# Cross-attention, two layers: the softmax shift's products of two key blocks and two heads in four groups of 32 rows

## What is computed

```
# layer 0: 16 heads of 64
h = layernorm(x, gamma, beta)
Q, K, V = h @ Wq, context @ Wk, context @ Wv
attn = softmax(Q K^T) * 64 ** -0.5
x = x + (attn V) @ Wo + bo
# layer 1: 16 heads of 32
xn = rmsnorm(x) * norm_w
q, k, v = rope and l2-normalise(xn @ wq, ctx @ wk), ctx @ wv
x = x + (softmax(q k^T * sqrt(32)) v) @ wout
```

## Time and profile before

| | us |
|---|---|
| median of 3 runs | 3376.78 |
| lowest and highest | 3375.62, 3377.91 |
| the profiled execution's own time | 3378.76 |
| its span | 3376.9 |
| TensorE busy | 3157.1 |
| VectorE busy | 2385.7 |
| ScalarE busy | 1404.2 |

### The profile page before, as it was taken

How to read it: one execution, slowest core, us unless ns; L and a number is a source line. 1 busy time by engine, 2 the same in 40 slices (tenths; PEclk the granted TensorE clock), 3 DMA queues, 4 the chain that set the end, 5 groups by cost and what they waited for, 6 DMA issues and landing times.

```text
span 3376.9 us, 51123 instructions
## 1 busy us (share of the span) xinstructions
PE 3157.1 (93%) x20448; PEld 1614.6 (48%) x20448; DVE 2385.7 (71%) x2805; ACT 1404.2 (42%) x1728; POOL 502.6 (15%) x221
## 2 busy tenths in 40 slices
PE   5999999899899999889999999998999999999897
PEld 3555555444355554544344555454434455545442
DVE  3667666787776676678776766667877767666877
ACT  1333333456433333355643333335563333334555
POOL 1000002342000000334100000034410000013440
PEclk8999999999999999999999999999999999999999
DMA  3001000101111010011111010101112010000001
GB/s 108 18 21 25 22 23 15 57 22 39 43 49 25 21 24 21 21 55 25 32 55 41 21 25 21 24 14 58 26 32 71 21 27 21 25 21 21 18 14 36
DMA packets 178322, 105.88 MB, mean 31 GB/s; under 512 B 81453, under 2 KB 147117, under 8 KB 178089
## 3 DMA queue, kind: packets, MB, share of 16 engines
q1 hardware_dynamic: 178088, 102.60, 11.4%
HBM read 93.12 MB, written 9.42 MB: 30 GB/s over the span
## 4 chain that ended last, share of the span: by engine, by line
PE 83%; DVE 8%; issue 4%; ACT 3%; DMA 1%; SPq 1%; DVEq 0%; POOL 0%; ACTq 0%; POOLq 0%
PE o_acc L654 19%; PE scores L642 19%; PE work L680 14%; PE work L676 11%; PE work L700 10%; PE work L610 5%; DVE acc L797 4%; PE work L694 3%; ACT probs L727 2%; DVE tile_max L778 1%; PE work L684 1%; DVE resid L882 1%; DVE stats L817 1%; PE work L710 0%; PE work L689 0%
## 5 line engine op out<-in xcount | busy, mean ns | idle before, releaser
L727 ACT ACTIVATE probs<-scores 128x1024 f32<-128x1024 f32 x1024 | 995.8, 1023 | 501.2 <-PE scores L642 462.1
L778 DVE TENSOR_REDUCE tile_max<-work 128x2 f32<-128x1024 f32 x496 | 607.0, 1224 | 557.4 <-PE work L610 554.0
L797 DVE TENSOR_TENSOR acc<-acc,probs 128x1024 f32<-128x1024 f32 x768 | 984.8, 1305 | 20.2 <-ACT probs L727 0.2
L654 PE MATMUL o_acc<-probs,v_tok 128*64 128x512 f32 (+1 forms) x4096 | 778.1, 611 | 0.1
L914 POOL TENSOR_TENSOR inv<-sumsq,power 128x16 f32<-128x16 f32 x64 | 233.0, 3640 | 2110.5 <-DVE sumsq L863 2110.5
L700 PE MATMUL work<-wo,o_sum 128*128 128x512 f32 x768 | 429.6, 647 | 39.7 <-issue 27.6
L642 PE MATMUL scores<-q_high,k_high 32*128 32x512 f16 (+1 forms) x2048 | 311.4, 394 | 71.0 <-ACT probs L727 47.3
L654 PEld LDWEIGHTS o_acc<-probs,v_tok 128*64 128x64 f32 (+1 forms) x4096 | 165.4, 122 | 349.1 <-issue 334.4
L882 DVE TENSOR_TENSOR resid<-work,resid 128x512 f32<-128x512 f32 x384 | 261.4, 684 | 65.3 <-PE work L700 65.2
L642 PE MATMUL scores<-q_high,k_low 32*128 32x512 f16 (+1 forms) x2048 | 305.4, 385 | 0.0
L642 PE MATMUL scores<-q_low,k_high 32*128 32x512 f16 (+1 forms) x2048 | 304.5, 384 | 0.0
(11 more groups left out here) (77 smaller groups left out, 2662.6 us busy)
## 6 DMA issues: line engine op xcount, KB each, us to landing
recip<-rows_dram SPq DMA_DIRECT2D x380, 64.0 KB, 2.1
stage<-in_x_dram SPq DMA_DIRECT2D x8, 1024.0 KB, 6.3
wq<-in_L_xattn_Wq_dram SPq DMA_DIRECT2D x32, 256.0 KB, 2.8
resid<-in_x_dram SPq DMA_DIRECT2D x8, 1024.0 KB, 5.4
wo<-in_L_xattn_Wo_dram SPq DMA_DIRECT2D x32, 256.0 KB, 2.7
out_dram<-resid SPq DMA_DIRECT2D x8, 1024.0 KB, 4.3
wk<-in_L_xattn_Wk_dram SPq DMA_DIRECT2D x32, 192.0 KB, 2.6
wv<-in_L_xattn_Wv_dram SPq DMA_DIRECT2D x32, 192.0 KB, 2.6
```

What stands on the lines that cost most here:

```text
L654: mm = pe.matmul(o_acc[h * d:(h + 1) * d, :], v_tok[par][:, kt, h * d:(h + 1) * d], probs[:, unit_slot(t, n, kt, h // 2), h % 2, :], start ...
L727: act.activation(probs[:, no % RING, :, :], scores[:, unit_banks(t, n, kt, u), :], ACT.Exp, scale=(1.0, float(D1) ** 0.5 / QK_SCALE ** 2)[ ...
L778: dve.tensor_reduce(tile_max[:, qt, :, n:n + 1], maxima_banks(e), AX.X, ALU.max, negate=True).then_inc(dve_freed, 1)
L797: dve.tensor_tensor(a[:, heads, :], before, probs[:, unit_slot(t, n, kt, u), :, :], ALU.add).then_inc(add_ok, 1)
```

## The change

In layer 0 the shift's products leave `products`. For every even block, that is once a step, `shift_pair` writes four of them ahead of the others: for block i (0 or 1) of the step and head h, rows 64h + 32i to 64h + 32i + 31 of `ones_r` and `shift`, into that block's and head's own bank. For this the row of `shift` with the maximum has to be there twice, at rows 0 and 32 and at rows 64 and 96; a second reduction on VectorE writes columns 32 and 96 of `neg_max`. The waits of both blocks for `exp_ok` stand ahead of the four products. Layer 1 is as before.

```
+            def shift_pair(t, n, kt):
+
+                for i in range(2):
+                    no = UNIT_NO[t, n, kt + i, 0]
+                    if no >= 2:
+                        pe.wait_ge(exp_ok, no - 1)
+                for i in range(2):
+                    for h in range(G0):
+                        r = slice(h * D0 + i * D1, h * D0 + (i + 1) * D1)
+                        pe.matmul(scores[:, 2 * (UNIT_NO[t, n, kt + i, 0] % 2) + h, :], ones_r[r, :], shift[t % 2][r, tokens(n)],
+                                  start=True, stop=False)
...
-                if units[-1] >= 2:
-                    pe.wait_ge(exp_ok, units[-1] - 1)
...
                 if l == 0:
-                    products = ((kh, qh), (kl, qh), (kh, ql), (None, shift[par]))
+                    if kt % 2 == 0:
+                        shift_pair(t, n, kt)
+                    products = ((kh, qh), (kl, qh), (kh, ql))
                 else:
+                    if units[-1] >= 2:
+                        pe.wait_ge(exp_ok, units[-1] - 1)
                     products = ((kh, qh), (kl, qh), (kh, ql), (kl, ql))
...
-                        k_rows = ones_r[r, :] if kk is None else kk[r, tile(kt)]
-                        mm = pe.matmul(scores[:, first + h, :], k_rows, qq[r, tokens(n)], start=(i == 0), stop=(i == len(products) - 1))
+                        mm = pe.matmul(scores[:, first + h, :], kk[r, tile(kt)], qq[r, tokens(n)], start=(l == 1 and i == 0),
+                                       stop=(i == len(products) - 1))
...
-                    dve.tensor_reduce(neg_max[:, :, 0:D0 + 1:D0], tile_max[:, :, :, :], AX.X, ALU.min).then_inc(neg_max_ok, 1)
+                    dve.tensor_reduce(neg_max[:, :, 0:D0 + 1:D0], tile_max[:, :, :, :], AX.X, ALU.min)
+                    dve.tensor_reduce(neg_max[:, :, D1:D0 + D1 + 1:D0], tile_max[:, :, :, :], AX.X, ALU.min).then_inc(neg_max_ok, 1)
```

## The result

The changed kernel takes 3412.34 us (median of 4 runs, 3410.57 to 3415.11) where the kernel before takes 3377.35: 1.0103 times as long, 95% interval 1.0086 to 1.0121. It is slower by 35 us; 3417 had been forecast, 40 more than before. The profiled execution took 3413.29 us, its span 3411.5.

A forecast was written before the change was run, and what follows sets the result against it. TensorE was taken as the bound in layer 0. Steps +38, wait +4.5, hidden -2 made +40.5 us; on the profiled 3378.76 that is 3419, 3417 us as median. Likeliest's range 3393 to 3436, whole range down to 3366.

The forecast's parts named there:

- What bounds the kernel: Layer 0's main part: TensorE works 414.03 of 420 us, so nearly every nanosecond counts; other engines have room.
- What is removed and added: Per layer 0 step, two shift pairs of 0.231 us go (0.46); four 32-row products side by side add 0.23.
- Two changes of shape, 0.20 each: Layer 0 scores, 64 rows to 32 and back: each way 0.10 us emptying plus 0.10 exposed load.
- The guess for the four's load: Weights of the four 32-row shift products: fp32r with 128 columns, 0.10 us exposed; lower bound 0.01 as in f16.
- Where it stands: +0.17 us at 228 of 256 steps, behind 64-row products; -0.03 at 28 behind 128 rows; together +38 us.
- The wait moved forward: First product awaits both exps; binds only at five places where two steps' scores adjoin, 0.9 us each, +4.5 us.
- VectorE's second reduction at nothing: Second reduction to neg_max, 64 times 0.172 us, 11 us of VectorE; covered, so nothing added.
- What hides some of it: Rowmax waits for VectorE's reduction, about ten of 19 in layer 0, hide longer scores: 2 us taken off.
- VectorE "has room": Layer 0 stretch of 420 us: VectorE works 287.70, leaving over 130 us of room for the second reduction.
- no emptying between 64 and 32 rows (A): Rival for layer 0's shape changes: type change caused layer 1's 0.10; each step gains 0.23, 3321 us; chance 0.17.
- one way free (B): Rival: one of the two shape changes costs nothing, -0.03 us a step, 3373 us; chance 0.09.
- two and two (D): Rival: the fp32r fours don't run four at once, taking 0.46; +0.40 us a step, 3483 us; chance 0.02.

The follow-up runs named there:

- The doubled four: The changed kernel with its four shift products run twice in a row, shape unchanged between them: 3473.1 us, 1.0284.
- the run in f16: The changed kernel with shift and its ones held in f16 instead of fp32r: 3398.19 us, 1.0059 times the kernel before.
- the run in f16 pairs: The kernel before with shift and its ones in f16, pairs of 64 rows left in their old place: 3378.25 us, 1.0002.

## Why the prediction was right

**What bounds the kernel:** right, TensorE in layer 0; nearly the whole of a longer step came through to the end.

**What is removed and added:** a pair 0.231, the four 0.23. The doubled four measured 0.24 a step. Right.

**Two changes of shape, 0.20 each:** right, and this was the step that decided. The Trainium skill, TensorEngine Tiling (Array Packing), Key Properties, says that a change of mode drains TensorE; the trace agrees for both ways, at 0.10 us each. 0.44 and 0.43 stand in the timeline where 0.43 and 0.43 were forecast, and 0.50 twice. The way back, for which no row existed without a wait, costs the same as the way in. The guess for the four's load, 0.10 as in fp32r and not 0.01 as in f16, was right too; the run in f16 shows the other.

**Where it stands:** 0.17 a step was forecast, medians show 2.361 - 2.189 = 0.172.

**The wait moved forward:** 4.5 us forecast, 5 us in the run that has only this.

**VectorE's second reduction at nothing:** the run allows 0 to 0.2%, so it was not shown to be exactly nothing.

**What hides some of it:** too small. The sum of steps and places is 42.5 and 35 were measured, so 7 to 8 are missing where 2 had been taken off. Summed from start to start over the traces, all rowmax took 18.4 us more, where 228 x 0.10 = 23 had been added; the output projections (L714) took 2.4 less and the products with `v_tok` 1.2 less. The waits for VectorE's reductions say the same, the answer to the earlier trace rows:

```profile
PE work L610 <- DVE tile_max L792: 22.0, 21, 1.9
```

27.2 before, 22.0 after. Not all of it need be hiding: the mean granted clock of the changed kernel's runs was 0.991, that of the kernel before 0.990, which by the fits above is 2 to 3 us. The two traces differ more (0.991 and 0.988), so their sums are rough by some us.

**VectorE "has room":** this was wrong, though the sum did not suffer, since the change lengthened what covers VectorE. The busy share of 287.70 in 420 us says that its throughput is free, not that its answers are in time. Halving the reduction won 41 us in the kernel before. Three things can be read from its trace. First, the waits of the earlier trace rows, 27.2 us, became:

```profile
PE work L610 <- DVE tile_max L778: 14.2, 14, 1.3
```

13 us less. Second, the load rows of TensorE: of the kernel before, the output projection's loads,

```profile
PEld work L700 <- DVE tile_max L778: 186.7, 216, 1.7
```

and with the halved reduction

```profile
PEld work L700 <- issue: 305.8, 371, 3.8
...
PEld work L700 <- DVE tile_max L778: 5.0, 6, 0.8
```

So VectorE released those loads last before, and no longer does. Most of that idle time is still there, now under "issue"; but from the last product with `v_tok` to the first of the output projection, 230 places in layer 0, the starts stand 127.7 us apart in all, where it was 137.6: some 10 us less. Third, the clock. The longest wait of the earlier trace rows, and what follows it, with the busy time of that stretch (the clock is the 0.51):

```profile
1790.56 0.80 PE L610 MATMUL work<-k_high,q_high 64*128 64x512 f32 x2 [2.44 <-DVE tile_max L778]
1791.28 3.68 PE L654 MATMUL o_acc<-probs,v_tok 128*64 128x512 f32 x8
...
1790.00:1797.00 7.00, 6.44 (x13) 2.13 (x14) 5.28 (x6) 0.00 (x0) 0.00 (x0) 0.51 0.00 0
```

and the same place with the halved reduction:

```profile
1766.56 0.41 PE L610 MATMUL work<-k_high,q_high 64*128 64x512 f32 x2
1766.90 1.94 PE L654 MATMUL o_acc<-probs,v_tok 128*64 128x512 f32 x8
```

TensorE stood idle for 2.44 us, and then for 7 us its clock was at the lower level (1.2 GHz) and the eight products took 3.68 us; without the idle time the clock stayed at 2.4 GHz and they took 1.94. So it looks as if a late answer of VectorE was paid twice there; one place is no proof of it. The page's tenths hide such short stretches. Over the runs the halving goes with a clock of 0.9925 for 0.9906, by the fits above 3 to 5 us. The three overlap and are no full account; the rest of the 41 us stays open.

**The rivals:** no emptying between 64 and 32 rows (A) falls by the timeline and by the run in f16 pairs; one way free (B) falls by the 0.43 and 0.50 behind the four; two and two (D) falls by the doubled four.

## What to carry to other kernels

A packing of small products is worth its saved stream less two changes of shape: here 0.23 us saved against 0.40 spent, so four products are too few, and two such fours in a row, each in the place of two pairs, would by these numbers only about break even (0.46 against 0.40, an estimate; no run has it). Count changes of the array's shape in the order of the instructions, put the small products where a change happens anyway, and then look for what was hidden behind the stretch that gets shorter: the next user of the same banks had only 0.4 us of slack. Whether an engine is in time is read in the start of the loads behind it, not in its busy share. And before a miss of some us is put down to a mechanism, compare the granted clocks: 0.001 of it went with 1.7 to 2.8 us here.

## What the runs showed of the hardware

Emptying costs about 0.10 us at each change of shape, and the load behind it shows 0.10 in fp32r of 128 columns and 0.01 in f16, also between 64 and 32 rows, in both directions. A change between fp32r and f16 at one shape costs nothing that 1024 of them a run could show (under 0.004 us each), but it shifts the recorded starts by some 0.19 us. A wait of 0.10 for a bank costs 0.20, since it also takes the load's cover away. An idle stretch of 2.44 us was followed by 7 us at half the clock.
